# Fused embedding, attention and expert layer on one core: five PSUM banks for units and two for scores, copies of q and k by transfers, value projections spread otherwise

## The reference

```python
h = concat(x @ W_tok + pe, text_embedding)          # (16, 1101, 128)
a = layernorm(h)
q, k, v = a @ wq[h], a @ wk[h], a @ wv[h]           # 8 heads of 64
o = softmax(q @ k.T / 8) @ v
h = h + concat_heads(o) @ head_kernel
f = layernorm(h) * scale + bias                      # then one group of 2, two experts of its 4
h = h + shared(f) + sum of the two chosen experts(f) # swiglu, width 256; float32 throughout
```

## Time and profile before

| | |
|---|---|
| median of 3 runs | 5187.49 us (5181.03 to 5187.82) |
| the profiled execution | 5181.64 us, of it a span of 5179.9 us |
| mean granted PE clock | 0.977 of full |
| PE busy | 4702.1 us (91%) |
| DVE, POOL, ACT busy | 3214.4, 2943.0, 2647.0 us |
| chain that ended last, PE's share | 69% |

### The profile page before, as it was taken

How to read it: one execution, slowest core, us unless ns; L and a number is a source line. 1 busy time by engine, 2 the same in 40 slices (tenths; PEclk the granted TensorE clock), 3 DMA queues, 4 the chain that set the end, 5 groups by cost and what they waited for, 6 DMA issues and landing times.

```text
span 5179.9 us, 94570 instructions
## 1 busy us (share of the span) xinstructions
PE 4702.1 (91%) x25829; PEld 3377.0 (65%) x25829; DVE 3214.4 (62%) x7726; ACT 2647.0 (51%) x6408; POOL 2943.0 (57%) x1803
## 2 busy tenths in 40 slices
PE   5999989999899998999999998998999989999997
PEld 3666666666666666666666666666666666666666
DVE  5556656566565666656566565665656656566654
ACT  2664554555545545545455455455455554555542
POOL 0775555555555565565555555555555555555662
PEclk7999999999999999999999999999999999999998
DMA  1000000000000000000000000000000000000000
GB/s 39 14 21 14 12 23 13 18 14 13 23 13 18 13 18 19 13 18 19 18 14 13 18 18 17 14 13 23 13 18 14 13 23 12 18 14 13 19 9 18
DMA packets 110624, 87.00 MB, mean 17 GB/s; under 512 B 69264, under 2 KB 101895, under 8 KB 110087
## 3 DMA queue, kind: packets, MB, share of 16 engines
q1 hardware_dynamic: 110087, 80.46, 5.5%
HBM read 59.63 MB, written 19.65 MB: 15 GB/s over the span
## 4 chain that ended last, share of the span: by engine, by line
PE 69%; ACT 10%; DVE 9%; issue 6%; DMA 2%; SPq 2%; POOL 0%; ACTq 0%; DVEq 0%; POOLq 0%
PE o_ps L832 21%; PE work L729 11%; PE work L788 8%; PE scores L813 8%; PE scores L815 8%; DVE part_max L986 3%; ACT probs L929 2%; PE work L749 2%; PE work L772 2%; PE work L740 2%; PE work L723 2%; ACT k_a L881 2%; DVE h_out L1030 2%; PE work L716 1%; DMA q_b<-max_rows 1%
## 5 line engine op out<-in xcount | busy, mean ns | idle before, releaser
L1215 POOL TENSOR_TENSOR sums<-sums,probs 128x736 f32<-128x736 f32 (+3 forms) x1344 | 2365.1, 1760 | 1178.1 <-ACT probs L929 1138.6
L929 ACT ACTIVATE probs<-scores 128x368 f32<-128x368 f32 (+3 forms) x3456 | 1459.5, 474 | 1571.9 <-PE scores L815 1534.1
L986 DVE TENSOR_REDUCE part_max<-work 128x1 f32<-128x368 f32 (+3 forms) x3456 | 1650.3, 530 | 597.5 <-PE work L729 585.4
L813 PE MATMUL scores<-q_a,k_a 128*128 128x368 f32 (+3 forms) x3456 | 1174.9, 340 | 133.0 <-DMA q_b<-max_rows 72.3
L832 PE MATMUL o_ps<-probs,values 128*64 128x368 f32 (+1 forms) x6912 | 1229.5, 491 | 0.0
L815 PE MATMUL scores<-q_b,k_b 128*128 128x368 f32 (+3 forms) x3456 | 1149.6, 333 | 0.0
L729 PE MATMUL work<-k_a,q_a 128*128 128x368 f32 (+3 forms) x3456 | 973.9, 363 | 46.0 <-ACT normed L891 26.6
L729 PEld LDWEIGHTS work<-k_a,q_a 128*128 128x128 f32 (+1 forms) x3456 | 593.8, 185 | 374.9 <-issue 232.2
L832 PEld LDWEIGHTS o_ps<-probs,values 128*64 128x64 f32 (+1 forms) x6912 | 460.5, 140 | 548.3 <-issue 448.7
L813 PEld LDWEIGHTS scores<-q_a,k_a 128*128 128x128 f32 (+1 forms) x3456 | 638.4, 185 | 231.1 <-issue 104.5
L1211 POOL TENSOR_TENSOR sums<-probs 128x736 f32<-128x736 f32 (+1 forms) x192 | 338.2, 1761 | 687.9 <-ACT probs L929 683.6
(11 more groups left out here) (185 smaller groups left out, 4915.3 us busy)
## 6 DMA issues: line engine op xcount, KB each, us to landing
sums<-inverse_rows SPq DMA_DIRECT2D x384, 92.0 KB, 2.7
resid_rows<-heads_t SPq DMA_DIRECT2D x16, 576.0 KB, 3.0
h_out<-resid_rows SPq DMA_DIRECT2D x16, 576.0 KB, 3.9
heads_t<-in_pe_table_dram SPq DMA_DIRECT2D x16, 512.0 KB
out_dram<-h_out SPq DMA_DIRECT2D x16, 512.0 KB
inv_cols<-sums SPq DMA_DIRECT2D x384, 1.4 KB
inverse_rows<-inv_cols SPq DMA_DIRECT2D x192, 2.9 KB
q_b<-max_rows SPq DMA_DIRECT2D x128, 4.0 KB
```

The costliest lines, as they stand in the source:

```text
L813: nc.tensor.matmul(o, k_a[p % 2][i][:, t * P:t * P + n], q_a[p % 2][i][:, c0:c0 + cw], start=True, stop=False)
L929: nc.scalar.activation(probs[0:n, slot(s), i, 0:cw], scores[0:n, h % SB, 0:cw], ACT.Exp, scale=DH ** -0.5).then_inc(probs_ready, 1)
L986: nc.vector.tensor_reduce(part_max[0:n, i * NT + j, c:c + 1], w[0:n, 0:keys], AX.X, ALU.max).then_inc(drained[k], 1)
L1215: nc.gpsimd.tensor_tensor(acc, acc, probs[0:n, slot(s), :, 0:cw], ALU.add).then_inc(sums_done, 1)
```

## The change

Three edits. `LANES` goes from 4 to 5 and `SB` from 3 to 2. ACT casts the high part once for each head (two casts for a `qk` unit), and SP copies it to its second place by two transfers of 64 rows of 368 elements, inside SBUF; SP waits for the casts first (`qk_hi`), and the first `max` units that read a part wait for its transfers (`qk_again`). The `v` units are spread by the load of DVE and ACT and not by PE's, which also moves experts' units, since they are laid out after them.

```diff
-LANES = 4
-SB = 3
+LANES = 5
+SB = 2
...
-EVEN_MAX, EVEN_V, EVEN_POST = (0, 1, 0), (1, 0, 0), (1, 0.5, 0)
+EVEN_MAX, EVEN_V, EVEN_POST = (0, 1, 0), (0, 1, 1), (1, 0.5, 0)
...
+    qk_again = {(what, c): sem(f"{what}_again{c}") for what in "kq" for c in range(NC)}
...
+                for _, _, what, part in max_needs.get(u, []):
+                    pe.wait_ge(qk_again[what, part], 32 * (qk_pair(b, p) + 1))
                 mm = nc.tensor.matmul(w[0:n, 0:cw], q_a[p % 2][i][:, j * P:j * P + n],
                                       k_a[p % 2][i][:, c0:c0 + cw], start=True, stop=True)
...
+                hi = k_a if what == "k" else q_b
                 for i in range(2):
-                    src = w[64 * i:64 * i + 64, 0:cw]
-                    a, z = (k_a, k_a) if what == "k" else (q_a, q_b)
-                    nc.scalar.copy(a[p % 2][i][0:64, c0:c0 + cw], src)
-                    o = 64 if what == "k" else 0
-                    nc.scalar.copy(z[p % 2][i][o:o + 64, c0:c0 + cw], src).then_inc(qk_hi, 1)
+                    nc.scalar.copy(hi[p % 2][i][0:64, c0:c0 + cw], w[64 * i:64 * i + 64, 0:cw]).then_inc(qk_hi, 1)
...
+                if u[0] == "qk":
+                    _, p, what, c = u
+                    c0, cw = CHUNKS[c]
+                    wait_then(sp.wait_ge, qk_hi, 12 * qk_pair(b, p) + 4 * c + 2 * "kq".index(what) + 2)
+                    for i in range(2):
+                        src = (k_a if what == "k" else q_b)[p % 2][i][0:64, c0:c0 + cw]
+                        to = k_a[p % 2][i][64:128, c0:c0 + cw] if what == "k" else q_a[p % 2][i][0:64, c0:c0 + cw]
+                        sp.dma_start(to.bitcast(F32), src.bitcast(F32)).then_inc(qk_again[what, c], 16)
```

More of the change, by code:

```diff
@@ L676, in run, with qk_pair @@
         iteration(epi, 0, B)
+    def qk_pair(b, p):
+        return PAIRS * b + (p - 1) % PAIRS + 1
     def item_of(b, q):
@@ L970, in unit @@
                 c0, cw = CHUNKS[c]
-                n = 12 * (PAIRS * b + (p - 1) % PAIRS + 1) + 4 * c + 2 * "kq".index(what)
+                n = 12 * qk_pair(b, p) + 4 * c + 2 * "kq".index(what)
                 for i in range(2):
```

## The result

The changed kernel takes **4881.34 us** (median of 4 runs, 4872.68 to 4882.34) against 5184.84 us for the kernel before on the same chip: a ratio of 0.9411, 95% interval 0.9395 to 0.9428. It is 303 us faster.

A forecast was written before the change was run, and what follows sets the result against it. The prediction took PE, busy 91% of the span, to bound the kernel. Its terms summed to -175.6 us, with 9 taken off -167, so 5181.6 becomes 5015 us, range 4965 to 5105.

The forecast's parts named there:

- Fifth bank: Ten PE waits for a unit's bank, 192.6 us in sum, go except 7 us of normed: -185.6 us; lower bound 93.
- Casts halved: ACT loses 22 us an item, counted only where PE waits for ACT, ahead of the scores at step 87: -9 us.
- Transfers' waits: First max waits for q's first chunk, 0.8 us each in the pairs at steps 27 and 81: +24; prologue +3.
- SP's queue: Sum and reciprocals at a pair's steps 3 and 5 stand behind up to 1.2 us of issues; costed at nothing.
- Two score banks: Score tiles wait for the exponential two tiles back, 0.35 us at step 13, about 0.4 at step 17: +12 us.
- Values: Moved v units and expert: -15 at the third pair's turning, +5 at step 106, -10 for the hid wait.
- The signs named: Profile signs: bank waits below 40 us, scores for probs 40 to 70, maxima's transfers 70 to 80, max waits at steps 3, 30, 84.
- first rival: The next wait takes over: PE gets ahead of DVE and half the bank term stays; 5108 at worst, 5075 middle; chance 0.20.
- more than the sum: Rival: max runs paced by DVE also gain from a bank, and waits for ACT shrink elsewhere: 4970; chance 0.13.
- The transfers land late: Rival: each us beyond 2.7 costs 45 to 60 us; with 1.5 us more, 5100; chance 0.12.
- Two score banks bind everywhere: Rival: 0.35 us lost at every step would be 567 us, making the kernel slower; chance 0.07.
- More half-clock stretches: Rival: new waits at steps 30 and 84 might each bring a 1.7 us slow-clock loss, 51 us, 5066; chance 0.08.

The follow-up runs named there:

- waits_only: no_transfers plus waits in PE's program, before the first max units that read a part, for ACT casts already done; 4832.67 us, ratio 0.9324.
- scores_two: The kernel before with two score banks instead of three and still four banks for units; 5205.86 us, ratio 1.0043.
- no_banks: The changed kernel with the old split of four banks for units and three for scores; 5042.65 us, ratio 0.9725.
- values_alone: The kernel before with only the value projections spread by the load of DVE and ACT; 5163.43 us, ratio 0.9962.
- no_transfers: The changed kernel without the q and k transfers and their waits; second copies hold a constant, so not the reference's results; 4803.17 us, ratio 0.9265.
- store_later: The changed kernel with the store of the previous item's output, and its wait, moved four steps later in SP's queue; 4895.55 us, ratio 0.9444.

## Why the prediction was wrong

By its own steps:

- *Fifth bank, -185.6*: right in its mechanism and near in size. Measured -163 in the presence of the copies and -211 in their absence. The lower bound of 93 was far too careful: in no run did half of it stay away.
- *Casts halved, -9*: **the step that failed.** "ACT isn't the bound, so this counts only where PE waits for ACT." I took ACT's 51% of the span for an answer and counted one place, step 87. But in steps 1 to 2 and 28 to 29, where q and k are projected, ACT was busy for 92% and 98% of the time. PE's idle time is shown behind the exponential at steps 1 to 2 (0.97 us), and behind DVE, which waits for ACT, at 28 to 29 (0.33 and 1.32 us, which the prediction had put down to the bank); part of the loss looks like busy PE. Measured: -161 us beside five banks. I had even written that many bank waits end with DVE's half of a chunk "which in turn waits for ACT's four casts", and then priced only the bank.
- *Transfers' waits, +24, with prologue +3*: too small by 51; measured +78. Of the lateness, step 30 cost 1.36 us an item (I had 0.8) and the pair at step 81 cost 0.48 (0.8). The pair at step 0 cost 1.67 (term 0: the wait of 1.33 was to turn into one of the same size, but without transfers it falls to 0.58, so the trade hid a gain of the casts). The rest, some 2 us an item at step 0, comes with the waits' own instructions, a term that the prediction didn't have and that no row of before could show.
- *Landing 2.7 us*: it was 2.1. The error was in my favour and small against the others.
- *SP's queue, 0*: nothing measured contradicts it. The lateness (49 us) fills the whole difference of 48.7 us between waits_only, which has none of SP's new issues, and the changed kernel.
- *Two score banks, +12*: +23 with four casts, +2 with two. It was costed beside ACT's load of before, though the same change halves that load. Of the two places one was right: step 13 is 0.40 us longer (0.35 forecast), step 17 only 0.08 (0.4 forecast). An item of scores_two is 0.84 us longer in sum, by gains and losses at steps 0 to 3, 25 to 27 and 82 to 87; the rest of its 23 us lies mostly in the first two items and the last. A wait for an exponential of another source is new at step 26, where it stands behind copies of values (timeline of the changed kernel):

```profile
1608.38 0.92 ACT L879 COPY values<-work 128x256 f32<-128x256 f32 x3
...
1609.17 0.88 ACT L933 ACTIVATE probs<-scores 128x366 f32<-128x366 f32 x2
...
1609.73 0.39 PE L820 MATMUL scores<-q_a,k_a 128*77 128x366 f32 x1 [2.03 <-ACT probs L933]
```

The values' spread brought this wait: no_banks and values_alone, with three score banks, have it too (2.16 and 2.14 us).

- *Values, -20 in sum*: -21. In values_alone the row for `neg_max` falls from 42.9 to 28.3, the 15 that were forecast, and the row for `hid` from 17.2 to 7.1, the 10. What the prediction didn't see cancels: the maxima's transfers are waited for 48.7 us in place of 72.3, the exponentials 82.8 in place of 60.6. So the sum is right partly by luck.
- *Taken off for waits that come up behind, 9*: with the banks alone these waits were much larger (102.7 and 46.1 above); in the full change the copies removed the first and the values' spread the second.
- *The signs named*: the bank waits (about 10 us, below 40) and the waits for `probs` (59.6, 40 to 70) came as said. The maxima's transfers did not (45.3, not 70 to 80), nor did `max` at step 3: it waits 0.84 to 0.90 us in the twelve items, not 1.5 to 2.5. At step 84 it waits 0.2 to 0.3 us, at step 30 in seven of the twelve items 1.15 to 1.94. In the first rival, 5075 isn't the middle of 5015 and 5108, which is 5062; nothing hangs on it.

The sum by measured steps in the full change's company: -163 - 161 + 78 + 2 - 21 = -265. The 38 us to -303 are the overlap of casts and banks, which shows in these figures since each is what is lost when that part alone is taken out of the full change. Of the rivals, "more than the sum" (4970) had the right sign and its reason was half of the cause: "waits for ACT shrink elsewhere". "The transfers land late" fell, they land in 2.1 us. "Two score banks bind everywhere" fell: the step of four exponentials lasts 1.06 us where it lasted 0.66, about as forecast, and all 108 steps together are 0.84 us longer in scores_two. "More half-clock stretches" is true of step 0 and not of the sum. At step 0 the clock is at half for 7.0 us an item where it was for 3.4, at step 3 for 0.6 where it was for 3.4; in all, slow stretches sum up to 243.5 us in the changed kernel, 240.5 before and 212.7 in no_transfers.

## What to carry to other kernels

Ask for the busy share of every engine in windows of two or three steps around the work that a change removes, before calling an engine "not the bound": ACT at 51% of the span was at 98% in the steps that counted. Where a wait names one engine and that engine waits for another, price the removal of work on the second too; and cost the parts of one change in each other's company. Keep the copy by transfer for parts that are needed late, and let the engine copy the part that is needed at once.

## What was not expected of the hardware

- A transfer of 64 rows by 1472 bytes inside SBUF lands 2.1 us after its issue (2.7 for the one from HBM), and in one item looked at SP takes 1.10 to 1.16 us to issue two of them.
- Six wait instructions a pair in PE's program, none of which holds anything up in the loop, cost 29.5 us (4803.17 to 4832.67), some 2 us an item at the loop's jump.
- An engine's waits can be shown wholly as "issue" there: 3.46 and 3.47 us in one step of store_later.
